# Additive attention on one core: other engines for the slots' relus, and a new order of scores, maxima and sums

## The chip, the cores and the metric

The kernel runs as one program on one core of a Trainium2 chip. The metric is device time in microseconds (us). PE is TensorE, DVE VectorE, ACT ScalarE, POOL GpSimd, SP SyncE.

## The reference, cut to what matters

The whole program is two layers of an adaLN network. The change touches only the attention of layer 1, on X of 4 batches x 1024 tokens x 256 channels, with 64 features (A = 64):

```python
q = jnp.einsum('bnc,ac->bna', X, Wq)
k = jnp.einsum('bnc,ac->bna', X, Wk)
Vy = jnp.einsum('bnc,dc->bnd', X, Wy_w) + Wy_b
e = jax.nn.relu(_rho_signed_sqrt(q[:, :, None, :] + k[:, None, :, :]))
scores = jnp.einsum('bija,a->bij', e, Wphi)
m = jnp.max(scores, axis=-1, keepdims=True)
ex = jnp.exp(scores - m)
denom = jnp.sum(ex, axis=-1)
part1 = jnp.einsum('bij,bjc->bic', ex, Vy)
Ew = jnp.einsum('bij,bija->bia', ex, e)
part2 = jnp.einsum('bia,ca->bic', Ew, We_w) + We_b * denom[..., None]
return (part1 + part2) / (denom[..., None] + EPS_DEN)
```

For every pair (i, j) of tokens and every feature, e is the root of the relu of q + k. It is used twice: for the scores, and, weighted with ex, for Ew.

## The kernel before

**Tiles and slots.** A tile is 32 queries (TI = 32) against all 1024 keys of the batch. It has 16 slots (NP = 16), each of two queries: partitions are 2 queries x 64 features, and a slot is 1024 keys wide. There are 128 tiles, four (q = 0 to 3) to a group of 128 queries, 32 to a batch. `e_slots` holds two tiles (`par` = q % 2). While tile t is worked on by DVE, tile t+1 gets its last roots and its scores, and tile t+2 gets its relus and first root.

**What each tile costs each engine.** The relu of a slot, relu(k + q), is made by the engine that `Z_BY` names: V, DVE in one instruction (L753, five slots, all issued in a burst behind slot 15 by `Z_AFTER`); A, ACT in one (L575, four slots); P, POOL in two, a clamp (L680) and an addition (L686), seven slots. A relu for tile t+2 overwrites the slot of tile t, so it waits for DVE's multiply of that slot. ACT then takes roots of four slots at a time (L584, four per tile; root s covers slots 4s to 4s+3 and waits for all four relus), and once per tile loads the exponential's table, takes ex from the scores and the negative maximum (L591), and loads the root's table again. POOL splits ex in two parts (`parts`, L666 and L668), which PE needs for all broadcasts of the next tile.

**PE and DVE, slot by slot.** PE's `tile` runs over the slots n of tile t: two matmuls broadcast ex (L493) into one of two PSUM buffers (`spread`), for which broadcast n waits for multiply n-2; then come the quarters of scores that `SCORES_AT[n]` lists, each 4 matmuls in 8 passes of 256 columns (L452). Quarters 4s to 4s+3 need root s. Entries `(1, ...)` are of tile t+1, `(2, ...)` of tile t+2. Once per tile PE turns ex (L499) at slot `EXT_AT` (0) or, for q = 0, at `EXT_AT_FIRST`; ACT copies it out (`turned`), for q = 0 DVE (L805). In q = 3 and the next q = 0, PE adds the group's eight products with the values, at the slots in `SUMS_LAST` and `SUMS_NEXT`; in q = 1 it turns the group's output back at slot `TURN_AT`, for which ACT's `normed` must have run. DVE multiplies slot by slot (L798, reads the broadcast and `e_slots`, and accumulates Ew), takes the maximum of tile t+1 in three steps behind slots `MAX_AT` to `MAX_AT + 2` (L760, L765, L770), ends a group in q = 0 and q = 1 (L778, L780, L786), and takes over the next batch's keys and queries at a seam (`next_batch`, three times in all).

Each engine runs its instructions in the order written; all waits are on semaphores (`sqrt_done`, `xb_freed`, `bc_done`, `scores_done`, `max_done`, `exp_done`, `parts_done`).

**Order in the loops.** ACT's step: root 3 of t+1, `turned`, relus of slots 2 and 3, root 0 and relu of slot 6 (all of t+2), exponential of t+1, relu of slot 10, roots 1 and 2 of t+2. POOL's step: queries of the tile (L690), relus in pairs (0, 1), (4, 5), (7, 8), `parts`, relu of slot 9.

Of the kernel before, what the change touches and what calls it, by code (L numbers as in the profile page):

```python
# [10 lines left out]
P = 128  # L11
# [27 lines left out]
NP = TI // 2  # L39
# [5 lines left out]
GT = 4  # L45
# [40 lines left out]
def adaln_kernel(nc, a, out):  # L86
# [9 lines left out]
    Z_BY = "PPAAPPAPPPAVVVVV"  # L96
    Z_AFTER = {15: [11, 12, 13, 14, 15]}


    EXT_AT, EXT_AT_FIRST, MAX_AT, TURN_AT = 0, 13, 8, 4  # L100

    SUMS_LAST, SUMS_NEXT = {9: 1, 14: 1, 15: 2}, {0: 1, 8: 1, 9: 1, 10: 1}
# [3 lines left out]
    SCORES_AT = {1: (1, (4, 5, 6, 7, 8)), 2: (1, (9,)), 3: (1, (10,)), 4: (1, (11,)), 5: (1, (12,)), 6: (1, (13,)), 7: (1, (14,)),  # L106
                 8: (1, (15,)), 10: (2, (0,)), 11: (2, (1,)), 12: (2, (2,)), 13: (2, (3,))}
    SCORES_AT_FIRST = SCORES_AT | {1: (1, (4, 5, 6, 7)), 2: (1, (8,)), 3: (1, (9, 10))}
# [18 lines left out]
    with ctx:  # L127
# [268 lines left out]
        TILES, GROUPS, N_SUMS = B * NTI, B * NG, JT  # L396
# [42 lines left out]
        def pe_c(pe):  # L439
# [45 lines left out]
            def tile(t, q, first=False, last=False, sums_of=None, values=None, more_sums_of=None, turn=None):  # L485
# [4 lines left out]
                for n in range(NP):  # L490
# [4 lines left out]
                    if n == (EXT_AT if q else EXT_AT_FIRST):  # L495
                        pe.wait_ge(ext_copied, t + 1)
                        for j in range(JT):
                            half, block = divmod(j, JT // BPB)
                            turned_ = nc.tensor.matmul(banks[:, 6, j * TI:(j + 1) * TI],  # L499
                                                       ex_parts[:, par, block * P:(block + 1) * P],  # L500
                                                       c_["selt"][:, half, :], start=True, stop=True)
                        turned_.then_inc(ext_mm, 1)
# [6 lines left out]
                    ahead, ms = (SCORES_AT if q else SCORES_AT_FIRST).get(n, (0, ()))  # L509
# [55 lines left out]
        def act_c(act):  # L565
# [26 lines left out]

            def first_root(t, par, freed):
                for n in (2, 3):
                    relu(t, par, n, freed)
                sqrt(t, par, 0)
                relu(t, par, 6, freed)

            def next_roots(t, par, freed):
                relu(t, par, 10, freed)  # L600
                nc.scalar.preload_act_table(ACT.Sqrt)  # L601
                sqrt(t, par, 1)
                sqrt(t, par, 2)

            def last_root(t, par):
                sqrt(t, par, 3)
# [6 lines left out]
            def turned(t, q):  # L613

                act.wait_ge(ext_mm, t + 1)
                nc.scalar.activation(ex_t_of[:, :, :, q, :], turned_ex, ACT.Copy).then_inc(ext_copied, 1)

            def step(t, q):

                par = q % 2  # L620
                last_root(t + 1, 1 - par)
                if q:
                    turned(t, q)
                first_root(t + 2, par, t * NP)
                ex_of(t + 1, 1 - par)
                next_roots(t + 2, par, t * NP)
# [4 lines left out]
            for n in (2, 3, 6):  # L631
                relu(1, 1, n, None)
            ex_of(0, 0)
            relu(1, 1, 10, None)
            nc.scalar.preload_act_table(ACT.Sqrt)
            for s in range(3):
                sqrt(1, 1, s)
            step(0, 0)
            step(1, 1)
            with act.Fori(0, GROUPS - 1) as tg:  # L640
                step(tg * GT + 2, 2)
                step(tg * GT + 3, 3)
                step(tg * GT + GT, 0)
                normed(tg)
                step(tg * GT + (GT + 1), 1)
            last_root(TILES - 1, 1)
            turned(TILES - 2, 2)
            ex_of(TILES - 1, 1)
# [12 lines left out]
        def pool_c(pool):  # L661
# [32 lines left out]
            pool.wait_ge(z_v, Z_BY.count("V"))  # L694
            pool.sem_inc(z_clamped, Z_BY.count("P"))
            some_z(1, 1, (0, 1), None)
            some_z(1, 1, (4, 5), None)
            parts(0, 0)
            some_z(1, 1, (7, 8), None)
            some_z(1, 1, (9,), None)  # L700

            def step(t, par, tl=None, last=False):

                if not last:
                    tile_queries(tl, par)
                    some_z(t + 2, par, (0, 1), t * NP)
                    some_z(t + 2, par, (4, 5), t * NP)
                    some_z(t + 2, par, (7, 8), t * NP)
                pool.wait_ge(bc_done, t * NP)
                parts(t + 1, 1 - par)  # L710
                if not last:
                    some_z(t + 2, par, (9,), t * NP)
# [18 lines left out]
        def dve_c(dve, own):  # L731
# [58 lines left out]
            def step(t, q, more=True, ends=None, seam=None, adds=None):  # L790

                par = q % 2
                if seam is not None:
                    next_batch(seam)
                for n in range(NP):
# [5 lines left out]
                    if ends is not None and n == EXT_AT_FIRST:  # L801
                        group_end(ends, 0)
                    if q == 0 and n == EXT_AT_FIRST + 1:
                        dve.wait_ge(ext_mm, t + 1)
                        nc.vector.tensor_copy(ex_t_of[:, :, :, q, :], turned_ex).then_inc(ext_copied, 1)  # L805
                    if MAX_AT <= n < MAX_AT + 3 and (more or q == GT - 2):
                        row_max(t + 1, 1 - par, n - MAX_AT, 0 if q else -1)
                    if ends is not None and n == EXT_AT_FIRST + 1:
                        group_end(ends, 1)
                    if adds is not None and n == TURN_AT + 2:  # L810
                        group_end(adds, 2)
# [1855 lines left out]
```

## Time and profile before

| | us |
|---|---|
| Median of 3 runs (5036.22 to 5052.96) | 5045.31 |
| Span of the profiled execution | 5032.0 |
| PE busy | 4414.1 (88%) |
| DVE busy | 4019.8 (80%) |
| ACT busy | 3419.9 (68%) |
| POOL busy | 3163.8 (63%) |
| Attention stage, first to last multiply | about 1230 to 4303 |

The span is the program on the chip; the runs' times are somewhat longer. A row of the costliest groups reads: line, engine, operation, output<-input, shapes, count | busy us in all, mean ns of one | idle time of the engine just before them, and what ended most of it. In a timeline, consecutive instructions of one engine overlap by some 0.08 us, so that what one costs is the distance between two starts; two starts follow from one another in the rows. In a table of stretches each engine has its busy us and, in brackets, its number of instructions; behind them stand the granted clock of PE (1.00 is 2.4 GHz) and the DMA. "x5" after a row is five instructions merged, with the time of all.

### The profile page before, as it was taken

The page shows a single profiled execution, that of the slowest core. Times are in us where ns is not written, and L with a number is a line of the kernel's source. Part 1 is how long each engine was busy: PE and PEld are TensorE (multiplying, and loading weights), DVE is VectorE, ACT ScalarE, POOL GpSimd, SP SyncE. Part 2 cuts the span into 40 slices and gives each one's busy share as a digit, 9 for nine tenths or more (in the row PEclk, how much of TensorE's full clock was granted, in tenths as well). Part 3 has the DMA queues.
Part 4 walks back from the last instruction along what each step waited for, and adds up shares of the span by engine and source line. Part 5 has one row for each costly group of instructions (what it writes and reads, how often), then busy time and mean ns, then how long its engine had stood idle before and what let it go on. Part 6 is the DMA issues. An engine that isn't in the chain of part 4 may idle for free.

```text
span 5032.0 us, 83939 instructions
## 1 busy us (share of the span) xinstructions
PE 4414.1 (88%) x28586; PEld 2295.6 (46%) x28586; DVE 4019.8 (80%) x6598; ACT 3419.9 (68%) x2402; POOL 3163.8 (63%) x2716
## 2 busy tenths in 40 slices
PE   6888876887889888888988988898898888799998
PEld 3333333464334433434433433443443443577777
DVE  2789896535999999999999999999999999422225
ACT  2232221315999999999999999999999999444443
POOL 0666662534777777777777777777777777233334
PEclk8888887899999999999999999999999999999999
DMA  6000001352000000000000000000000000200002
GB/s 229 0 0 1 0 1 51 134 175 89 3 2 2 4 2 2 17 4 2 2 4 2 17 4 2 2 4 2 11 3 4 2 2 4 102 17 8 17 25 84
DMA packets 70482, 130.78 MB, mean 26 GB/s; under 512 B 8264, under 2 KB 46632, under 8 KB 65889
## 3 DMA queue, kind: packets, MB, share of 16 engines
q1 hardware_dynamic: 61152, 106.21, 6.2%
q0 software_dynamic: 9216, 23.17, 1.2%
q8 instruction: 58, 0.95, 0.1%
q14 instruction: 56, 0.45, 0.0%
HBM read 74.66 MB, written 61.03 MB: 27 GB/s over the span
## 4 chain that ended last, share of the span: by engine, by line
PE 30%; issue 23%; DVE 15%; ACT 14%; POOL 2%; DVEq 1%; DMA 0%; ACTq 0%; POOLq 0%; SPq 0%
ACT e_slots L584 11%; PE banks L2250 8%; PE banks L493 8%; DVE e_slots L798 7%; PE banks L452 7%; DVE e_slots L753 2%; ACT L601 1%; DVE ew L798 1%; POOL g_l L2380 1%; PE banks L1602 1%; ACT e_slots L575 1%; PE banks L465 1%; PE banks L289 1%; PE banks L1656 1%; PE banks L1553 1%
## 5 line engine op out<-in xcount | busy, mean ns | idle before, releaser
L798 DVE CUSTOM_DVE_ANT_0 e_slots<-e_slots,banks 128x1024 f32<-128x1024 f32 x2048 | 2445.5, 1217 | 101.9 <-PE banks L493 97.4
L584 ACT ACTIVATE e_slots<-e_slots 128x4096 f32<-128x4096 f32 x512 | 1841.0, 3620 | 72.1 <-DVE e_slots L753 43.0
L493 PE MATMUL banks<-ex_parts,sel 128*128 128x512 f32 x4096 | 1513.5, 452 | 165.5 <-DVE ew L798 156.2
L680 POOL TENSOR_SCALAR e_slots<-k,qt 128x1024 f32<-128x1024 f32 x889 | 993.6, 1119 | 686.5 <-DVE ew L798 628.5
L452 PE MATMUL banks<-e_slots,w_score 128*32 128x256 f32 x16384 | 1249.9, 397 | 167.2 <-ACT e_slots L584 160.8
L493 PEld LDWEIGHTS banks<-ex_parts,sel 128*128 128x128 f32 x4096 | 628.7, 189 | 905.8 <-DVE ew L798 732.7
L686 POOL TENSOR_SCALAR e_slots<-e_slots,qt 128x1024 f32<-128x1024 f32 x889 | 988.7, 1119 | 63.9 <-POOL e_slots L680 25.5
L452 PEld LDWEIGHTS banks<-e_slots,w_score 128*32 128x32 f32 x16384 | 374.5, 110 | 861.7 <-issue 560.6
L575 ACT ACTIVATE e_slots<-k,qt 128x1024 f32<-128x1024 f32 x508 | 565.9, 1139 | 3.4 <-DVE ew L798 3.3
L2380 POOL TENSOR_TENSOR g_l<-tmp,g_h 128x512 fp32r<-128x512 f32 x192 | 260.6, 1358 | 421.2 <-ACT g_h L2347 288.4
L753 DVE TENSOR_SCALAR e_slots<-k,qt 128x1024 f32<-128x1024 f32 x635 | 453.3, 779 | 0.0
L2250 PE MATMUL banks<-g_h,r_h 128*128 128x512 f32 x1024 | 406.6, 397 | 6.4 <-POOL g_l L2380 6.4
L1283 POOL TENSOR_TENSOR state<-state,r_ 128x1024 f32<-128x1024 f32 x128 | 294.3, 2302 | 184.7 <-DVE state L1383 183.9
L2250 PE MATMUL banks<-g_l,r_h 128*128 128x512 f32 x1024 | 400.3, 391 | 0.0
L1383 DVE TENSOR_TENSOR_SCAN state<-decay,banks 128x1024 f32<-128x1024 f32 x128 | 292.3, 2284 | 4.4
L2346 ACT ACTIVATE tmp<-banks,r_sh 128x512 f32<-128x512 f32 x128 | 88.3, 690 | 269.8 <-PE banks L2250 269.7
L2250 PEld LDWEIGHTS banks<-g_h,r_h 128*128 128x128 f32 x1024 | 193.3, 189 | 51.3 <-POOL g_l L2380 9.0
L591 ACT ACTIVATE ex<-banks,negmax 128x512 f32<-128x512 f32 x128 | 88.2, 689 | 184.9 <-DVE negmax L770 184.9
L2250 PEld LDWEIGHTS banks<-g_l,r_h 128*128 128x128 f32 x1024 | 193.4, 189 | 43.3 <-issue 3.4
L2405 DVE RECIPROCAL r_std<-r_std 128x512 f32<-128x512 f32 x7 | 23.5, 3353 | 218.8 <-ACT r_std L2314 218.8
L668 POOL TENSOR_TENSOR ex_parts<-ex,part 128x512 fp32r<-128x512 f32 x128 | 164.3, 1283 | 10.7
L1013 PE MATMUL banks<-v_parts,spread 128*128 128x512 f32 x256 | 112.7, 528 | 65.9 <-DVE state L1383 65.1
(341 smaller groups left out, 5006.4 us busy)
## 6 DMA issues: line engine op xcount, KB each, us to landing
stage<-in_h SPq DMA_DIRECT2D x16, 1024.0 KB, 4.8
moe_slots<-empty_slot SPq DMA_DIRECT2D x1, 10320.0 KB, 36.2
slots<-moe_slots SPq DMA_DIRECT2D x8, 1290.0 KB, 6.9
moe_out<-empty_slot SPq DMA_DIRECT2D x1, 8192.0 KB, 56.4
two_rows<-moe_out SPq DMA_DIRECT2D x16, 512.0 KB, 5.8
stage<-in_w SPq DMA_DIRECT2D x6, 1024.0 KB, 6.3
x_tokens<-in_x SPq DMA_DIRECT2D x1, 4096.0 KB, 18.9
w_down<-in_w_down SPq DMA_DIRECT2D x1, 4096.0 KB, 12.9
```

The lines of the kernel that those rows point to most:

```text
L452: ins = nc.tensor.matmul(banks[TI * g:TI * (g + 1), par, side * QW:(side + 1) * QW], c_["w_score"][:, s, half, :], e_slots[:, par, COLG * ...
L493: ins = nc.tensor.matmul(spread[n % 2][:, half * W:(half + 1) * W], c_["sel"][:, half, n, :], ex_parts[:, par, :], start=True, stop=True)
L575: nc.scalar.activation(e_slots[:, par, n, :], k2[:, :], ACT.Relu, bias=qt[:, par, 0, place(n):place(n) + 1]).then_inc(z_a, 1)
L584: nc.scalar.activation(e_slots[:, par, four, :], e_slots[:, par, four, :], ACT.Sqrt, bias=EPS_RHO).then_inc(sqrt_done, 1)
L680: nc.gpsimd.tensor_scalar(e_slots[:, par, n, :], k2[:, :], FLT_MAX, qt[:, par, 1, place(n):place(n) + 1], ALU.min, ALU.max).then_inc(z_cla ...
L686: nc.gpsimd.tensor_scalar(e, e, qt[:, par, 0, place(n):place(n) + 1], 1.0, ALU.add, ALU.mult).then_inc(z_p, 1)
L753: nc.vector.tensor_scalar(e_slots[:, par, n, :], k2[:, :], qt[:, par, 0, place(n):place(n) + 1], 0.0, ALU.add, ALU.max).then_inc(z_v, 1)
L798: nc.vector.tensor_tensor_reduce(out=e, in0=e, in1=spread[n % 2], scale=1.0, scalar=0.0, op0=ALU.mult, op1=ALU.add, accum_out=ew[:, q, pla ...
L1283: nc.gpsimd.tensor_tensor(state, state, r_[:, b % 2, n // N, :], ALU.mult).then_inc(pr_done, 1)
L1383: nc.vector.tensor_tensor_scan(st[:, s % RING, 1:T + 1], dk[:, c, :], kv, 0.0, ALU.mult, ALU.add).then_inc(scan_done, 1)
L2250: ins = nc.tensor.matmul(dst, w_[w][:, k, o * P:(o + 1) * P], x[:, k, :], start=k == 0 and part_ == 0, stop=k == n_k - 1 and part_ == 1)
L2380: nc.gpsimd.tensor_tensor(w_[lo][:, o, :], tmp[:, o % N_TMP, :], w_[hi][:, o, :].bitcast(fp32), ALU.subtract).then_inc(lo_done, 1)
```

## The change

Seven relus stay with POOL, four with ACT and five with DVE, but on other slots: POOL 0, 1, 3, 4, 6, 9, 15; ACT 2, 5, 7, 14; DVE 8, 10, 11, 12, 13 (still one burst behind slot 15). POOL makes them in threes (0, 1, 3), (4, 6, 9), then `parts`, then 15. ACT takes only root 1 behind the exponential; roots 2 and 3, with relu 14 between them, come in the next step, behind `turned` and, where there is one, `normed`. The maxima go from behind slots 8, 9, 10 to 10, 11, 12. The scores of t+1 end at slot 10 instead of 8, those of t+2 come at slots 12, 13 and 15, and slots 0, 2, 6, 11 and 14 have none. The eight sums, the turning for q = 0, the turning back and DVE's group ends move, and the batch's hand-over goes behind slot 4. PE waits for the next tile's maximum before it turns ex in q = 0.

```diff
-    Z_BY = "PPAAPPAPPPAVVVVV"
-    Z_AFTER = {15: [11, 12, 13, 14, 15]}
-    EXT_AT, EXT_AT_FIRST, MAX_AT, TURN_AT = 0, 13, 8, 4
-    SUMS_LAST, SUMS_NEXT = {9: 1, 14: 1, 15: 2}, {0: 1, 8: 1, 9: 1, 10: 1}
-    SCORES_AT = {1: (1, (4, 5, 6, 7, 8)), 2: (1, (9,)), 3: (1, (10,)), 4: (1, (11,)), 5: (1, (12,)), 6: (1, (13,)), 7: (1, (14,)),
-                 8: (1, (15,)), 10: (2, (0,)), 11: (2, (1,)), 12: (2, (2,)), 13: (2, (3,))}
-    SCORES_AT_FIRST = SCORES_AT | {1: (1, (4, 5, 6, 7)), 2: (1, (8,)), 3: (1, (9, 10))}
+    Z_BY = "PPAPPAPAVPVVVVAP"
+    Z_AFTER = {15: [8, 10, 11, 12, 13]}
+    EXT_AT, EXT_AT_FIRST, MAX_AT, TURN_AT, SEAM_AT = 0, 14, 10, 1, 4
+    SUMS_LAST, SUMS_NEXT = {1: 1, 2: 1, 12: 1, 14: 1, 15: 3}, {11: 1}
+    SCORES_AT = {1: (1, (4, 5, 6, 7)), 3: (1, (8,)), 4: (1, (9,)), 5: (1, (10,)), 7: (1, (11,)), 8: (1, (12,)), 9: (1, (13,)),
+                 10: (1, (14, 15)), 12: (2, (0,)), 13: (2, (1,)), 15: (2, (2, 3))}
...
                         pe.wait_ge(ext_copied, t + 1)
+                        if not q:
+                            pe.wait_ge(max_done, t + 2)
...
-                    ahead, ms = (SCORES_AT if q else SCORES_AT_FIRST).get(n, (0, ()))
+                    ahead, ms = SCORES_AT.get(n, (0, ()))
...
+            def late_roots(t, par, freed):
+                sqrt(t, par, 2)
+                relu(t, par, 14, freed)
+                sqrt(t, par, 3)
+
             def first_root(t, par, freed):
-                for n in (2, 3):
+                for n in (2, 5):
                     relu(t, par, n, freed)
                 sqrt(t, par, 0)
-                relu(t, par, 6, freed)
-
-            def next_roots(t, par, freed):
-                relu(t, par, 10, freed)
+                relu(t, par, 7, freed)
+
+            def second_root(t, par):
                 nc.scalar.preload_act_table(ACT.Sqrt)
                 sqrt(t, par, 1)
-                sqrt(t, par, 2)
...
                 par = q % 2
-                last_root(t + 1, 1 - par)
                 if q:
                     turned(t, q)
+                if done is not None:
+                    normed(done)
+                late_roots(t + 1, 1 - par, (t - 1) * NP if not isinstance(t, int) or t else None)
                 first_root(t + 2, par, t * NP)
                 ex_of(t + 1, 1 - par)
-                next_roots(t + 2, par, t * NP)
+                second_root(t + 2, par)
...
                     tile_queries(tl, par)
-                    some_z(t + 2, par, (0, 1), t * NP)
-                    some_z(t + 2, par, (4, 5), t * NP)
-                    some_z(t + 2, par, (7, 8), t * NP)
+                    some_z(t + 2, par, (0, 1, 3), t * NP)
+                    some_z(t + 2, par, (4, 6, 9), t * NP)
                 pool.wait_ge(bc_done, t * NP)
                 parts(t + 1, 1 - par)
                 if not last:
-                    some_z(t + 2, par, (9,), t * NP)
+                    some_z(t + 2, par, (15,), t * NP)
...
-                if seam is not None:
-                    next_batch(seam)
                 for n in range(NP):
...
+                    if seam is not None and n == SEAM_AT:
+                        next_batch(seam)
-                    if ends is not None and n == EXT_AT_FIRST:
+                    if ends is not None and n == MAX_AT + 2:
                         group_end(ends, 0)
-                    if q == 0 and n == EXT_AT_FIRST + 1:
+                    if q == 0 and n == EXT_AT_FIRST:
...
-                    if ends is not None and n == EXT_AT_FIRST + 1:
+                    if ends is not None and n == EXT_AT_FIRST:
                         group_end(ends, 1)
-                    if adds is not None and n == TURN_AT + 2:
+                    if adds is not None and n == TURN_AT:
                         group_end(adds, 2)
```

## Rows read from the trace of the kernel before

**Rows 1.** The page's part 5: costliest groups of instructions, columns as described above.

```profile
L798 DVE CUSTOM_DVE_ANT_0 e_slots<-e_slots,banks 128x1024 f32<-128x1024 f32 x2048 | 2445.5, 1217 | 101.9 <-PE banks L493 97.4
...
L584 ACT ACTIVATE e_slots<-e_slots 128x4096 f32<-128x4096 f32 x512 | 1841.0, 3620 | 72.1 <-DVE e_slots L753 43.0
...
L680 POOL TENSOR_SCALAR e_slots<-k,qt 128x1024 f32<-128x1024 f32 x889 | 993.6, 1119 | 686.5 <-DVE ew L798 628.5
```

**Rows 2.** Busy time of each engine in one group of four tiles.

```profile
core 0: us, PE busy (x) PEld busy (x) DVE busy (x) ACT busy (x) POOL busy (x), PEclk, DMA share, GB/s
2525.00:2620.80 95.80, 84.99 (x696) 38.47 (x696) 93.32 (x170) 88.22 (x49) 72.14 (x68) 1.00 0.01 3
```

**Rows 3.** Timeline of DVE: start us, us, instruction, [idle before <-releaser]; next group's copy.

```profile
2221.01 0.42 DVE L805 COPY ex_t<-banks 128x256 f32<-128x256 f32 x1
```

**Rows 4.** Timeline of DVE, from a tile's five relus to the next tile's.

```profile
2150.75 3.42 DVE L753 TENSOR_SCALAR e_slots<-k,qt 128x1024 f32<-128x1024 f32 x5
...
2154.09 1.21 DVE L798 CUSTOM_DVE_ANT_0 e_slots<-e_slots,banks 128x1024 f32<-128x1024 f32 x1
...
2156.80 1.22 DVE L798 CUSTOM_DVE_ANT_0 e_slots<-e_slots,banks 128x1024 f32<-128x1024 f32 x1 [0.36 <-PE banks L493]
...
2165.34 0.69 DVE L760 TENSOR_REDUCE half_max<-banks 128x1 f32<-128x512 f32 x1
...
2165.95 1.21 DVE L798 CUSTOM_DVE_ANT_0 e_slots<-e_slots,banks 128x1024 f32<-128x1024 f32 x1
...
2168.29 0.15 DVE L770 TENSOR_TENSOR negmax<-half_max,banks 128x1 f32<-128x1 f32 x1
...
2169.50 1.22 DVE L798 CUSTOM_DVE_ANT_0 e_slots<-e_slots,banks 128x1024 f32<-128x1024 f32 x1
...
2170.64 1.22 DVE L798 CUSTOM_DVE_ANT_0 e_slots<-e_slots,banks 128x1024 f32<-128x1024 f32 x1
...
2174.07 3.73 DVE L753 TENSOR_SCALAR e_slots<-k,qt 128x1024 f32<-128x1024 f32 x5
```

**Rows 5.** Timeline of DVE in the tiles q = 0 and q = 1.

```profile
2124.07 1.22 DVE L798 CUSTOM_DVE_ANT_0 e_slots<-e_slots,banks 128x1024 f32<-128x1024 f32 x1 [0.73 <-PE banks L493]
...
2125.22 0.42 DVE L805 COPY ex_t<-banks 128x256 f32<-128x256 f32 x1
...
2139.22 0.61 DVE L786 SCALAR_TENSOR_TENSOR xg<-banks,gate_g,xg 128x128 f32<-128x128 f32 x2
```

**Rows 6.** Timeline of PE: broadcasts (L493), quarters of scores (L452).

```profile
2108.64 1.07 PE L452 MATMUL banks<-e_slots,w_score 128*32 128x256 f32 x16
...
2127.55 1.93 PE L452 MATMUL banks<-e_slots,w_score 128*32 128x256 f32 x32
...
2131.36 0.64 PE L452 MATMUL banks<-e_slots,w_score 128*32 128x256 f32 x8 [1.87 <-ACT e_slots L584]
...
2131.93 0.73 PE L493 MATMUL banks<-ex_parts,sel 128*128 128x512 f32 x2
...
2132.59 0.64 PE L452 MATMUL banks<-e_slots,w_score 128*32 128x256 f32 x8
```

**Rows 7.** Timeline of ACT: two exponentials in a row, a table load between.

```profile
2145.22 0.69 ACT L591 ACTIVATE ex<-banks,negmax 128x512 f32<-128x512 f32 x1 [1.61 <-DVE negmax L770]
...
2146.96 1.28 ACT L601 ACT_TABLE_LOAD   x1
...
2168.54 0.69 ACT L591 ACTIVATE ex<-banks,negmax 128x512 f32<-128x512 f32 x1 [1.20 <-DVE negmax L770]
```

**Rows 8.** Timeline of DVE, then POOL, at the start of the stage.

```profile
1213.98 3.40 DVE L753 TENSOR_SCALAR e_slots<-k,qt 128x1024 f32<-128x1024 f32 x5
...
1214.48 4.98 POOL L680 TENSOR_SCALAR e_slots<-k,qt 128x1024 f32<-128x1024 f32 x2 [16.47 <-DVE e_slots L831]
```

**Rows 9.** Timeline of POOL in the loop, and at a batch's end.

```profile
2170.77 1.28 POOL L668 TENSOR_TENSOR ex_parts<-ex,part 128x512 fp32r<-128x512 f32 x1
...
2174.55 0.66 POOL L690 COPY qt<-q_pairs 128x32 f32 x1
...
2730.96 0.21 POOL L690 COPY qt<-q_pairs 128x32 f32 x1 [5.20 <-DVE q_pairs L744]
```

More of the change, by code:

```diff
@@ L591, in ex_of @@
                 nc.scalar.activation(ex[:, :], bank(par), ACT.Exp, bias=negmax[:, 0:1]).then_inc(exp_done, 1)
+            def late_roots(t, par, freed):
+                sqrt(t, par, 2)
+                relu(t, par, 14, freed)
+                sqrt(t, par, 3)
             def first_root(t, par, freed):
-                for n in (2, 3):
+                for n in (2, 5):
                     relu(t, par, n, freed)
                 sqrt(t, par, 0)
-                relu(t, par, 6, freed)
-            def next_roots(t, par, freed):
-                relu(t, par, 10, freed)
+                relu(t, par, 7, freed)
+            def second_root(t, par):
                 nc.scalar.preload_act_table(ACT.Sqrt)
                 sqrt(t, par, 1)
-                sqrt(t, par, 2)
-            def last_root(t, par):
-                sqrt(t, par, 3)
             def normed(tg):
@@ L616, in turned, with step @@
                 nc.scalar.activation(ex_t_of[:, :, :, q, :], turned_ex, ACT.Copy).then_inc(ext_copied, 1)
-            def step(t, q):
+            def step(t, q, done=None):
                 par = q % 2
-                last_root(t + 1, 1 - par)
                 if q:
                     turned(t, q)
+                if done is not None:
+                    normed(done)
+                late_roots(t + 1, 1 - par, (t - 1) * NP if not isinstance(t, int) or t else None)
                 first_root(t + 2, par, t * NP)
                 ex_of(t + 1, 1 - par)
-                next_roots(t + 2, par, t * NP)
+                second_root(t + 2, par)
             for s in range(PER):
                 sqrt(0, 0, s)
-            for n in (2, 3, 6):
+            for n in (2, 5, 7):
                 relu(1, 1, n, None)
             ex_of(0, 0)
-            relu(1, 1, 10, None)
             nc.scalar.preload_act_table(ACT.Sqrt)
-            for s in range(3):
+            for s in range(2):
                 sqrt(1, 1, s)
@@ L643, in act_c @@
                 step(tg * GT + GT, 0)
-                normed(tg)
-                step(tg * GT + (GT + 1), 1)
-            last_root(TILES - 1, 1)
+                step(tg * GT + (GT + 1), 1, done=tg)
             turned(TILES - 2, 2)
+            late_roots(TILES - 1, 1, (TILES - 3) * NP)
             ex_of(TILES - 1, 1)
@@ L694, in pool_c @@
             pool.wait_ge(z_v, Z_BY.count("V"))
+            pool.wait_ge(z_p, Z_BY.count("P"))
             pool.sem_inc(z_clamped, Z_BY.count("P"))
-            some_z(1, 1, (0, 1), None)
-            some_z(1, 1, (4, 5), None)
+            some_z(1, 1, (0, 1, 3), None)
+            some_z(1, 1, (4, 6, 9), None)
             parts(0, 0)
-            some_z(1, 1, (7, 8), None)
-            some_z(1, 1, (9,), None)
+            some_z(1, 1, (15,), None)
             def step(t, par, tl=None, last=False):
```

## The prediction

> **What bounds the kernel now.** I read the timelines of one group of four tiles, engine by engine, because the shares of the whole span mix stages. The group repeats: DVE's copy of the turned ex comes at 2125.22 and again at 2221.01 [rows 3, 5], a round of 95.8 us. Counting the maxima over the stage gives the same 95.8 for all groups but three at 97.2 (PE at a lower clock for some microseconds) and three with a batch's end (1.3 to 2.8 more). In one such group DVE is busy 93.3 us, ACT 88.2, PE 85.0, POOL 72.1, at full clock [rows 2]. DVE is the bound, though not a perfect one: its multiplies stand idle 101.9 us in all, 97.4 of it for PE's broadcasts [rows 1], and gaps under a tenth of a microsecond come on top. They show as pace: back to back four multiplies take 2174.07 - 2169.50 = 4.57, so 1.143 each [rows 4]; beside PE slots with a broadcast and a quarter of scores the pace is PE's, 2132.59 - 131.36 = 1.23 [rows 6].
>
> Two things make PE late. First, behind slot 1 it stands at the quarter that needs root 2: 1.87 us in vain [rows 6], then DVE waits at slot 2 (0.36 in [rows 4]). Second, quarters in seven slots running let PE fall back 0.09 a slot. In q = 0 PE's turning of ex at slot 13, right behind DVE, adds 0.73 [rows 5], and in q = 1 the turning back comes on top of a slot that already has a quarter.
>
> **The bare DVE round.** 16 multiplies x 1.143 = 18.28. The maximum costs 2165.95 - 2165.34 = 0.61 and its two small steps 0.07 each (they overlap their neighbours): 0.75. The burst costs 2154.09 - 2150.75 = 3.34 [rows 4]. Sum 22.37 a tile, 89.5 a group. Group ends add 0.5 (two additions, 0.61 long), 0.34 (copy, 0.42 long) and 0.15 (two small ones, estimate) [rows 5]: 90.5. So 5.3 of 95.8 is loss, of which the change can take away all or nothing. The counts per engine (7, 4, 5 relus, 4 roots) stay, so the sum of DVE's work doesn't move; only the loss does.
>
> **Part 1, roots 2 and 3 behind `turned`; scores thinned out.** I walk a tile of q = 2 or 3, with 0 at DVE's first multiply. Multiply 10 starts at 10 x 1.143 = 11.4; behind it come the maximum (1.14 + 0.61), multiply 11, the small step, multiply 12 (each 1.14 + 0.07), so the negative maximum runs from 15.5 to 15.7 and the exponential starts at 15.77 (today 2168.54 - 2168.29 = 0.25 behind the last step's start [rows 4, 7]). ACT: table, root 1 (3.62, 3.53 from start to start) done at 21.3; `turned`; root 2 done at 25.1, that is 2.7 in the next tile; relu 14; root 3 done at 7.4; relus 2 and 5; root 0 starts at 9.7, done 13.2; relu 7; table; ready at 15.7. ACT's round without waits is 2168.54 - 2145.22 - 1.20 = 22.12 today [rows 7]; with relu 14 between two roots I take 22.2, so it fits in 22.37 with 0.1 to 0.2 to spare (q = 1 adds `normed`, about 0.36, but DVE has 0.5 more there). PE: quarters 4 to 7 start with root 1 at 21.3 and take 1.9 [rows 6], done at 23.2; broadcast 2 may start at 23.6 anyway. Quarter 8 is met at 3.1 (root 2: 2.7), quarter 12 at 8.8 (root 3: 7.4), quarter 0 at 13.7 (root 0: 13.2). No root is late, so PE's wait of 1.87 is gone, and DVE's wait at slot 2 with it.
>
> Broadcast n+2 may start 0.06 behind multiply n's end and needs 0.77 to DVE's start, so PE may be 0.24 late before DVE notices. This room is an estimate from the distances in the timelines. Three quarters in a row make 3 x 0.09 = 0.27, and a free slot (0.66 for the broadcast) resets it: 0.03 lost behind slots 5 and 9. The double quarter at slot 10 (1.0, from 1.07 in [rows 6]) lies beside the maximum's 0.61: none lost. In q = 0 the turning at slot 14 (0.8) loses about 0.06, where now it is 0.73. The new wait for `max_done` there has the next broadcast queued behind it, but the maximum is done at 15.8 and PE comes at 16.4: nothing. The three sums at slot 15 and the turning back at slot 1 lie beside the burst (3.34): nothing; without that cover 1.0 and 0.5. Group: 90.5 + 4 x 0.06 + 0.06 = 90.8. If my 0.24 of room is not there, each run of three costs its 0.27: 0.54 a tile, group 92.7.
>
> **Part 2, POOL's threes and slot 15.** Relu 15 can't start before multiply 15, which is when DVE's burst starts. Such a clamp stands in the trace once: given at 1214.48 beside DVE's burst of 1213.98 to 1217.38, two clamps took 4.98 instead of 2.24, so the first ended at 1218.35, 0.97 behind the burst, while the burst kept its 3.40 [rows 8]. So I take: POOL waits out the burst, DVE loses nothing. Then from the burst's end: rest of clamp 1.0, gap 0.2, addition 1.1, queries and gaps 0.45, three clamps 3.33, gap 0.1, three additions 3.33: 9.5. Root 0 wants them at 9.7. It fits by 0.2. The second three ends at 16.4, the exponential at 16.5; `parts` 16.7 to 18.75; DVE's burst starts at 19.0, POOL's slack 0.3. POOL's round is then full, where the clamps stood idle 686.5 us [rows 1]. Today POOL's addition for slot 9 runs into the burst and holds its first relu up, 3.73 instead of 3.42 for five [rows 4]; that 0.3 goes in most tiles and is already in the bare round.
>
> The Trainium skill, "SBUF — State Buffer", section "Who interferes with whom", says that DVE in a 2-port mode (its `tensor_scalar` can be one) and GpSimd exclude each other, and that whoever issues first has the shared ports for the whole instruction. It speaks of one instruction, not of a burst of five: by it POOL's clamp might come in between two relus. The clamp of the start did not.
>
> **Part 3, seams and ends.** The hand-over behind slot 4 (three times; today POOL waits 5.20 for it, [rows 9]) starts POOL's threes at 7.9 instead of 3 or so; root 0 and the exponential come some 3.5 late, and so does the next tile: 1.5 + 3.2 = 4.7 each, 14 in all against 6.9 now: +7. At the stage's start POOL makes six relus before the first `parts` instead of four, about +4.5, of which the first tiles give most back: +1.
>
> **Sum.** 31 groups x (95.8 - 90.8) = 155; -155 + 8 = -147. On the profiled execution 5032 - 147 = 4885; the median stands 13 above that span: 4898. Ends: without any PE loss (90.5) -164 + 8, 4889, and a few less if the groups of 97.2 go: 4880. With 0.54 a tile, -96 + 8: 4957.
>
> **Rivals.**
> A, POOL and ACT late (a new wait for the removed one). Slacks of 0.1 to 0.3 in three places are less than one gap of POOL. If the clamp behind the burst costs a whole unit more (1.1), POOL's chain burst, slots 0, 1, 3, root 0, exponential, `parts`, next burst is 18.6 + 3.3 + 1.1 = 23.0: 0.6 more a tile, 2.5 a group, 31 x 2.5 = 78: 4976. For: the chain is closed and 21.9 long already. Against: [rows 8] measures the delay.
> B, slower: POOL gets in between DVE's relus. Its place is the burst, in every tile. POOL's copy of the queries, waiting at the first relu, needed 0.66 instead of 0.21 [rows 9], so it came in behind one relu; if the clamp (1.11) and the addition (1.12) do likewise, the burst grows by 2.2. Group 90.8 + 8.9 = 99.7, 31 x 3.9 = 121, + 8: 5174. The clamp alone: 95.3, about 5038. It decides for slower from 1.3 us a tile of POOL's work inside the burst. Against: the clamp of [rows 8], the same instruction. That is what the page's rule would give if locks were handed over at each instruction.
> C, PE's waits move and don't shrink: a root misses its quarter by half a microsecond (0.4 to 0.5 of room at quarters 8 and 0), each time 0.3 to 0.5 for DVE: up to 1 a tile, 5022 (124 back).
>
> **How the numbers follow.** Forecast (4880 to 4957) 0.65; A 0.17; C 0.07; B with both instructions 0.06, with the clamp alone 0.05. The likeliest is 4898. Range 4875 to 4980: it takes in A and leaves out C and B, 0.18 together. A measurement of this kernel can't tell less than 0.3% (15 us). Slower: B with both 0.06, 0.01 of the rest; within: B's clamp alone and a third of C, 0.06; faster 0.87.
>
> **What would show it.** Right: a group round near 91; no wait of PE for L584 behind slot 1; DVE's multiplies idle under 25 us in all; the clamp of slot 15 some 4 us long behind the burst; the burst at 3.4. A shows as ACT's root 0 waiting for POOL and no wait of the exponential for the maximum; B as a burst of 5 us or more; C as PE waiting for L584. The prediction is wrong if `parts` slips behind the burst's start: it then waits out the whole burst, and the next tile starts some 2 us late.

## The result, and the profile after

The changed kernel takes 5166.82 us (median of 4 runs, 5155.82 to 5175.6) against 5049.14 (5036.22 to 5059.44): ratio 1.0238, 95% interval 1.0218 to 1.0258. It is slower by 118 us, where 147 us less were forecast. The profiled execution has a span of 5163.0 us against 5032.0.

From the page, the busy line and three groups (line, engine, operation, count | busy us, mean ns of one | idle before, releaser), which answer to [rows 1]:

```profile
PE 4455.2 (86%) x28586; PEld 2326.0 (45%) x28586; DVE 4160.2 (81%) x6598; ACT 3438.4 (67%) x2402; POOL 3240.4 (63%) x2716
...
L796 DVE CUSTOM_DVE_ANT_0 e_slots<-e_slots,banks 128x1024 f32<-128x1024 f32 x2048 | 2391.6, 1213 | 79.4 <-PE banks L492 78.4
...
L681 POOL TENSOR_SCALAR e_slots<-k,qt 128x1024 f32<-128x1024 f32 x889 | 1032.0, 1163 | 670.1 <-DVE ew L796 623.4
...
L753 DVE TENSOR_SCALAR e_slots<-k,qt 128x1024 f32<-128x1024 f32 x635 | 649.2, 1086 | 0.0
```

PE's lateness did go down: the idle time before DVE's multiplies fell from 101.9 to 79.4 us. But DVE's own relus (L753), 635 before and after, now take 649.2 us, 1086 ns each by the page; the same 635 took 453.3 us before, 779 each. This is the engine that bounds the stage. The round of one group of four tiles, from DVE's copy of the turned ex to the next, in the form of [rows 2]:

```profile
core 0: us, PE busy (x) PEld busy (x) DVE busy (x) ACT busy (x) POOL busy (x), PEclk, DMA share, GB/s
2240.90:2340.00 99.10, 86.28 (x697) 39.34 (x697) 97.64 (x170) 88.77 (x49) 74.60 (x69) 0.98 0.01 3
```

99.1 us instead of 95.8, with DVE busy 97.6 of it. DVE's timeline, which answers to [rows 4]:

```profile
2293.19 5.12 DVE L753 TENSOR_SCALAR e_slots<-k,qt 128x1024 f32<-128x1024 f32 x5
...
2298.24 1.21 DVE L796 CUSTOM_DVE_ANT_0 e_slots<-e_slots,banks 128x1024 f32<-128x1024 f32 x1
...
2303.46 1.22 DVE L796 CUSTOM_DVE_ANT_0 e_slots<-e_slots,banks 128x1024 f32<-128x1024 f32 x1 [0.58 <-PE banks L492]
...
2305.37 1.22 DVE L796 CUSTOM_DVE_ANT_0 e_slots<-e_slots,banks 128x1024 f32<-128x1024 f32 x1 [0.68 <-PE banks L492]
```

A burst of five is 5.12 us long instead of 3.42 (3.73 where POOL's addition ran into it). And POOL beside it, which answers to [rows 8, 9]:

```profile
2293.50 1.42 POOL L681 TENSOR_SCALAR e_slots<-k,qt 128x1024 f32<-128x1024 f32 x1 [0.61 <-DVE ew L796]
...
2295.12 1.33 POOL L687 TENSOR_SCALAR e_slots<-e_slots,qt 128x1024 f32<-128x1024 f32 x1 [0.20 <-POOL e_slots L681]
...
2296.40 0.66 POOL L691 COPY qt<-q_pairs 128x32 f32 x1
```

The clamp comes 0.31 us behind the burst's start and takes 1.42, not some 4; the addition takes 1.33. So POOL is not kept out: it comes in between the relus, twice. Taken one by one in the trace, the relus start at 0, 0.67, 2.20, 3.73 and 4.38 us, and the second and third last 1.61 each instead of 0.75. Each of POOL's two instructions costs DVE 0.87. All 126 bursts of the loop look like this one.

The last two rows of DVE are a second effect, in one tile of most groups. PE's timeline of that place and two stretches of the group (columns as above):

```profile
2299.51 0.74 PE L492 MATMUL banks<-ex_parts,sel 128*128 128x512 f32 x2 [1.95 <-DVE ew L796]
...
2301.32 0.96 PE L451 MATMUL banks<-e_slots,w_score 128*32 128x256 f32 x8
...
2302.20 1.22 PE L492 MATMUL banks<-ex_parts,sel 128*128 128x512 f32 x2
...
2303.36 1.08 PE L451 MATMUL banks<-e_slots,w_score 128*32 128x256 f32 x8
```

```profile
2297.50:2301.00 3.50, 1.15 (x8) 0.60 (x4) 3.50 (x7) 3.50 (x2) 1.31 (x2) 1.00 0.00 0
2301.00:2304.40 3.40, 3.40 (x21) 0.90 (x19) 2.82 (x5) 3.29 (x2) 2.14 (x3) 0.57 0.00 0
```

PE stands idle 1.95 us beside the longer burst; less than two microseconds later a quarter of scores takes 0.96 to 1.08 instead of 0.64 and a broadcast 1.22 instead of 0.73, at a granted clock of 0.57 on the mean, between full speed (2.4 GHz) and half (1.2 GHz). Such a tile is 25.5 us long instead of 24.1.

The sum fits the measured round: 90.8 as forecast for the new order, + 4 x 1.70 = 97.6, + 1.45 for that tile = 99.05; measured 99.1. Over 31 groups that is 31 x 8.3 = 257 us on top of the 147 less: +110, against 131 between the spans. Of the 21 us that are left, 10 don't belong to the change: DVE's first relu of the stage comes at 1213.46 instead of 1203.38, and over all runs of this study this moment lies between 1201 and 1215, behind the same code. So two spans should not be compared more closely than that. Most of the rest is six groups of 101.1 to 101.4 us with a granted clock of 0.95, where the kernel before has three of 97.2 to 97.3 between its seams. The three groups with a seam are 6.2, 4.6 and 4.6 longer than their neighbours, 1.4, 2.8 and 2.8 before: 8.4 more, of which 7 are in the forecast already.

### The profile page after: what moved, and what is told of

Same layout as the page of the kernel before. It is cut to its first block, busy times and chain, and to the rows that moved or that the text cites. A ratio compares the mean times of both kernels' runs of the same rounds, so it can differ in the third digit from the quotient of the medians.

```text
span 5163.0 us, 83882 instructions
## 1 busy us (share of the span) xinstructions
PE 4455.2 (86%) x28586; PEld 2326.0 (45%) x28586; DVE 4160.2 (81%) x6598; ACT 3438.4 (67%) x2402; POOL 3240.4 (63%) x2716
## 4 chain that ended last, share of the span: by engine, by line
DVE 44%; issue 19%; PE 17%; POOL 3%; DVEq 1%; ACT 1%; DMA 0%; POOLq 0%; SPq 0%; ACTq 0%
DVE e_slots L796 27%; DVE e_slots L753 10%; PE banks L2250 6%; PE banks L492 2%; DVE ew L796 2%; POOL g_l L2380 2%; PE banks L451 2%; PE banks L1602 1%; DVE half_max L760 1%; PE banks L288 1%; PE banks L1553 1%; PE banks L1656 1%; PE banks L1665 1%; DVEq L794 0%; PE banks L1587 0%
## 5 line engine op out<-in xcount | busy, mean ns | idle before, releaser
L796 DVE CUSTOM_DVE_ANT_0 e_slots<-e_slots,banks 128x1024 f32<-128x1024 f32 x2048 | 2391.6, 1213 | 79.4 <-PE banks L492 78.4
L681 POOL TENSOR_SCALAR e_slots<-k,qt 128x1024 f32<-128x1024 f32 x889 | 1032.0, 1163 | 670.1 <-DVE ew L796 623.4
L451 PE MATMUL banks<-e_slots,w_score 128*32 128x256 f32 x16384 | 1207.8, 396 | 73.2 <-ACT e_slots L585 73.1
L492 PEld LDWEIGHTS banks<-ex_parts,sel 128*128 128x128 f32 x4096 | 640.6, 193 | 1149.3 <-DVE ew L796 930.5
L687 POOL TENSOR_SCALAR e_slots<-e_slots,qt 128x1024 f32<-128x1024 f32 x889 | 1010.3, 1148 | 51.2 <-POOL e_slots L681 25.5
L451 PEld LDWEIGHTS banks<-e_slots,w_score 128*32 128x32 f32 x16384 | 392.8, 110 | 725.0 <-issue 482.2
L753 DVE TENSOR_SCALAR e_slots<-k,qt 128x1024 f32<-128x1024 f32 x635 | 649.2, 1086 | 0.0
```

What stands on the lines that cost most here:

```text
L451: ins = nc.tensor.matmul(banks[TI * g:TI * (g + 1), par, side * QW:(side + 1) * QW], c_["w_score"][:, s, half, :], e_slots[:, par, COLG * ...
L492: ins = nc.tensor.matmul(spread[n % 2][:, half * W:(half + 1) * W], c_["sel"][:, half, n, :], ex_parts[:, par, :], start=True, stop=True)
L681: nc.gpsimd.tensor_scalar(e_slots[:, par, n, :], k2[:, :], FLT_MAX, qt[:, par, 1, place(n):place(n) + 1], ALU.min, ALU.max).then_inc(z_cla ...
L687: nc.gpsimd.tensor_scalar(e, e, qt[:, par, 0, place(n):place(n) + 1], 1.0, ALU.add, ALU.mult).then_inc(z_p, 1)
L753: nc.vector.tensor_scalar(e_slots[:, par, n, :], k2[:, :], qt[:, par, 0, place(n):place(n) + 1], 0.0, ALU.add, ALU.max).then_inc(z_v, 1)
L796: nc.vector.tensor_tensor_reduce(out=e, in0=e, in1=spread[n % 2], scale=1.0, scalar=0.0, op0=ALU.mult, op1=ALU.add, accum_out=ew[:, q, pla ...
```

## The experiments

All times are medians; the kernel before took 5039.74 to 5042.96 beside them. The diffs are against the changed kernel, unless said otherwise.

### POOL behind the burst, and other arrivals

```diff
                 if not last:
+                    pool.wait_ge(z_v, (t + 3) * Z_BY.count("V"))
+                    pool.sem_inc(pool_begun, 1)
                     some_z(t + 2, par, (15,), t * NP)
```

> The change, but POOL's relu of slot 15 waits until all five relus of DVE's burst are done. Theory T (POOL's two instructions enter DVE's burst, and each holds it up 0.87 us): the burst is back at 3.4 us instead of 5.12, the group round falls from 99.1 us to 91 to 92.5, the time to 4890 to 4960. Rival A (POOL's chain is too long: the change would be slow without the collision, too): burst 3.4 us, but root 0 waits for POOL, group 93.5 or more, time 4980 or more. Rival K (the tile in each group with PE at half clock is a cost of the new order itself): it stays, 1.45 us a group, 45 us in all.

Measured: 4898.75 us (ratio to before 0.9713, 0.9689 to 0.9737). One group, and the burst, POOL's clamp and ACT's root 0:

```profile
2327.29:2418.32 91.03, 84.27 (x704) 39.17 (x696) 90.68 (x170) 88.34 (x49) 70.63 (x69) 1.00 0.01 3
```

```profile
2421.81 3.40 DVE L755 TENSOR_SCALAR e_slots<-k,qt 128x1024 f32<-128x1024 f32 x5
...
2425.61 1.12 POOL L681 TENSOR_SCALAR e_slots<-k,qt 128x1024 f32<-128x1024 f32 x1 [4.02 <-DVE e_slots L755]
...
2435.30 3.63 ACT L585 ACTIVATE e_slots<-e_slots 128x4096 f32<-128x4096 f32 x1 [0.68 <-POOL e_slots L687]
```

The burst is back at 3.40, the round 91.0, and the tile at half clock is gone from all but six of the 31 groups (PE's clock 1.00 in the others). Theory T holds, and the collision with what follows from it is worth 268 us. ACT waits for POOL before root 0 (0.68 us), as rival A had it, but that wait is nearly covered (91.0 against 90.8 in the next kernel): the chain has just room enough.

Left out altogether:

```diff
                 if not last:
-                    some_z(t + 2, par, (15,), t * NP)
+                    pool.wait_ge(xb_freed, t * NP + (15 + 3))
+                    pool.sem_inc(z_clamped, 1)
+                    pool.sem_inc(z_p, 1)
```

> The change without POOL's relu of slot 15 (that slot keeps stale data; its two counts are raised behind multiply 15). No collision and 2.2 us less work on POOL in each tile. Theory T: group 90.8 to 91.2, time 4890 to 4910; the difference to the kernel in which POOL waits out the burst is what that wait costs. Rival A: as fast as T here, but the kernel that waits is over 60 us slower.

Measured: 4887.45 us; a group takes 90.79, the forecast's 90.8. Waiting out the burst costs 11 us by the medians, 31 x 0.24 = 7 by the groups.

Then the question why POOL was kept out at the start of the stage [rows 8] and not here. First, the waits within the burst, and an additional clamp of slot 0 that doesn't wait for DVE's first relus:

```diff
-                if freed is not None:
-                    dve.wait_ge(xb_freed, freed + (n + 3))
-                dve.wait_ge(qt_ready, t + 1)
+                if n == Z_AFTER[15][0]:
+                    dve.wait_ge(qt_ready, t + 1)
+                    if freed is not None:
+                        dve.wait_ge(xb_freed, freed + (15 + 3))
...
+            pool.wait_ge(qt_ready, 2)
+            nc.gpsimd.tensor_scalar(e_slots[:, 1, 0, :], k2[:, :], FLT_MAX, qt[:, 1, 1, place(0):place(0) + 1],
+                                    ALU.min, ALU.max).then_inc(warm, 1)
+            pool.wait_ge(warm, 1)
+            pool.sem_inc(pool_begun, 1)
             pool.wait_ge(z_v, Z_BY.count("V"))
```

> The change, but only the first relu of DVE's burst has waits (for multiply 15 and the queries), the other four follow without any; and at the stage's start POOL makes one more clamp of slot 0, before it waits for DVE's first relus. Theory W (at the start of the stage POOL was kept out of a burst because the relus there had no wait on the multiplies): the burst is 3.4 us again, POOL's clamp some 4 us long, time about 4900 to 4960. Theory I (POOL gets in behind any relu that it finds running): the burst stays 5.1 us, time 5150 to 5180. For the start: if the 3.85 us of the first clamp was the wait for the burst, the clamp that comes second stays at 3.8 us; if it was a first use, the additional clamp takes that time and the second one 1.1 to 1.5 us, and then it lies inside the burst.

Measured: 5182.93 us, the burst 5.1: theory W falls. The start of the stage, DVE and POOL:

```profile
1202.69 11.55 DVE L838 TENSOR_SCALAR e_slots<-k,qt 128x1024 f32<-128x1024 f32 x16 [7.08 <-POOLq L280]
...
1214.16 3.40 DVE L760 TENSOR_SCALAR e_slots<-k,qt 128x1024 f32<-128x1024 f32 x5
...
1202.93 1.49 POOL L697 TENSOR_SCALAR e_slots<-k,qt 128x1024 f32<-128x1024 f32 x1 [5.59 <-POOLq L280]
...
1214.54 6.18 POOL L681 TENSOR_SCALAR e_slots<-k,qt 128x1024 f32<-128x1024 f32 x3 [10.12 <-DVE e_slots L838]
```

The additional clamp comes 0.24 us behind the first of 16 relus and gets in behind it (1.49 us; DVE's 16 take 11.55 instead of 10.69, as they do in the kernel that waits out the burst: the 0.87 again). The next one comes at the seventeenth relu and is kept out over the four that follow: three clamps 6.18 us. So neither a first use nor the waits explain [rows 8].

Then the moment at which POOL comes. In the first kernel one wait and two raised semaphores more delay it:

```diff
                 if not last:
+                    pool.wait_ge(xb_freed, t * NP + (15 + 3))
+                    for _ in range(2):
+                        pool.sem_inc(pool_begun, 1)
                     some_z(t + 2, par, (15,), t * NP)
```

> The change, but POOL raises a semaphore twice more between its wait for multiply 15 and its clamp, so that the clamp comes some 0.2 us later than the 0.30 us behind the start of DVE's first relu at which it comes in the change. Theory P (whether POOL gets in hangs on where in the running relu it comes: at 0.20 to 0.31 us behind its start it gets in behind it, at 0.38 to 0.53 us, as at the start of the stage in three kernels, it is kept out to the end of the burst): burst 3.4 us, clamp about 4 us long, time 4885 to 4910. Rival (in the loop POOL always gets in behind the relu it finds running): burst 5.1, time 5150 to 5180.

Measured: 5166.95 us. Burst, clamp and addition:

```profile
2296.12 5.13 DVE L756 TENSOR_SCALAR e_slots<-k,qt 128x1024 f32<-128x1024 f32 x5
...
2296.62 1.23 POOL L681 TENSOR_SCALAR e_slots<-k,qt 128x1024 f32<-128x1024 f32 x1 [0.81 <-DVE ew L799]
...
2298.05 1.32 POOL L687 TENSOR_SCALAR e_slots<-e_slots,qt 128x1024 f32<-128x1024 f32 x1 [0.20 <-POOL e_slots L681]
```

The clamp comes 0.50 us into the first relu and still goes in behind it, and 0.50 is also what lay between relu and clamp in [rows 8]: theory P falls. The next three let POOL wait for the first, the second or the third relu:

```diff
                 if not last:
+                    pool.wait_ge(z_v, (t + 2) * Z_BY.count("V") + 1)
+                    pool.sem_inc(pool_begun, 1)
                     some_z(t + 2, par, (15,), t * NP)
```

> The change, but POOL's clamp of slot 15 waits for the first relu of DVE's burst, so that it comes about 0.3 us behind the start of the second. Theory P: it gets in behind the second one, and its addition behind the third: burst 5.1 us, time 5150 to 5190. Rival (POOL gets in only behind a burst's first relu): burst 3.4 us, time 4885 to 4910.

Measured: 5190.61 us, from two executions that lie far apart (5164.8 and 5216.43; the trace is of the first). In the other two the 1 is a 2 and a 3. They were put on record together: "the kernel before this one" is the one that waits for the third relu, and theory Q is stated with that one.

> As the kernel before this one, but POOL waits for the second relu and comes during the third. Theory Q: it gets in behind the fourth, only the fifth is held up: burst 4.3 us, group 91.0 + 4 x 0.87 = 94.5, time 5000 to 5020, more if tiles at the lower clock come back. Rival (behind any running relu): the fourth and the fifth are held up, burst 5.1, 5150 to 5180. Rival (kept out from here on): 4885 to 4900.

Measured: 4985.01 us.

> The change, but POOL's clamp of slot 15 waits for the third relu of DVE's burst, so that it comes during the fourth. Theory Q (POOL waits for those of DVE's relus that are already handed on when it comes, and DVE hands them on ahead: at its first relu none, at the second one more, deep in a long burst several): the fifth is ahead of it, the burst stays 3.4 us, the clamp ends about 1.0 us behind the burst; time 4885 to 4900, if anything a little under the 4898.75 us of the kernel that waits for all five. Rival (only the relu that runs is waited for): the fifth is held up, burst 4.3 us, 0.87 a tile, 5000 to 5020.

Measured: 4880.38 us (ratio to before 0.9687, 0.9664 to 0.9711). The bursts and POOL's clamps of the three, in this order:

```profile
2303.45 5.05 DVE L755 TENSOR_SCALAR e_slots<-k,qt 128x1024 f32<-128x1024 f32 x5
...
2304.59 1.83 POOL L681 TENSOR_SCALAR e_slots<-k,qt 128x1024 f32<-128x1024 f32 x1 [1.45 <-DVE e_slots L755]
```

```profile
2299.04 4.18 DVE L755 TENSOR_SCALAR e_slots<-k,qt 128x1024 f32<-128x1024 f32 x5
...
2300.85 1.83 POOL L681 TENSOR_SCALAR e_slots<-k,qt 128x1024 f32<-128x1024 f32 x1 [2.58 <-DVE e_slots L755]
```

```profile
2304.01 3.40 DVE L755 TENSOR_SCALAR e_slots<-k,qt 128x1024 f32<-128x1024 f32 x5
...
2306.47 1.83 POOL L681 TENSOR_SCALAR e_slots<-k,qt 128x1024 f32<-128x1024 f32 x1 [2.77 <-DVE e_slots L755]
...
2308.51 1.13 POOL L687 TENSOR_SCALAR e_slots<-e_slots,qt 128x1024 f32<-128x1024 f32 x1 [0.20 <-POOL e_slots L681]
```

Coming 1.14 us behind the burst's start, in the second relu, POOL is done at 2.97, so it began at 1.86 (1.11 earlier), when the third relu was half through: one relu went ahead of it, the third, and the fourth was held up by 0.78. Its addition holds up the fifth by 0.87. Coming in the third it waits for the fourth and holds up only the fifth, by 0.78 (4.18). Coming in the fourth it waits for the fifth, and nothing is held up (3.40). Theory Q fits what was seen in all of these: ahead of POOL goes what DVE has already handed on, which is a reading and not measured. Measured is the number of relus that go ahead beyond the running one: none at a burst's first, one at the second and third, at least one at the fourth (the burst has no sixth), at least four at the seventeenth. What in DVE sets this number wasn't tested. The time of the kernel that came third (4985 against 5000 to 5020 expected) is under the range, because only 0.78 and not 0.87 is lost per tile, and on top of a round of 90.8 and not 91.0: 93.9 a group and not 94.5.

The kernel in which POOL waits for the third relu is the best of this study, 162 us faster than the kernel before. Its round and groups:

```profile
2322.87:2413.65 90.78, 84.38 (x702) 39.02 (x696) 90.59 (x170) 88.14 (x48) 73.44 (x69) 1.00 0.01 3
```

```profile
L798 DVE CUSTOM_DVE_ANT_0 e_slots<-e_slots,banks 128x1024 f32<-128x1024 f32 x2048 | 2384.8, 1214 | 31.3 <-PE banks L492 30.7
...
L585 ACT ACTIVATE e_slots<-e_slots 128x4096 f32<-128x4096 f32 x512 | 1851.4, 3623 | 51.3 <-POOL e_slots L687 27.3
...
L755 DVE TENSOR_SCALAR e_slots<-k,qt 128x1024 f32<-128x1024 f32 x635 | 431.9, 747 | 0.0
```

### The collision put into the kernel before

```diff
                 if not last:
+                    pool.wait_ge(xb_freed, t * NP + (15 + 3))
+                    pool.sem_inc(pool_begun, 1)
                     some_z(t + 2, par, (9,), t * NP)
```

> The kernel before, but POOL's last relu (slot 9) waits for multiply 15, so that its clamp and addition fall on DVE's burst. Theory T: burst 5.1 us instead of 3.4 to 3.7, 1.5 us a tile more, 126 tiles: 190 us, less what the longer burst takes off the waits for roots (up to 1 us in the tiles q = 1 to 3): 5120 to 5240. Rival (the collision costs only together with the new order): under 5070.

Measured: 5470.1 us, 428 more than before and far above what was expected. The burst is 5.12 here as well, but that is the smaller part. ACT and PE:

```profile
2304.38 7.12 ACT L584 ACTIVATE e_slots<-e_slots 128x4096 f32<-128x4096 f32 x2 [2.16 <-POOL e_slots L686]
...
2308.05 1.08 PE L452 MATMUL banks<-e_slots,w_score 128*32 128x256 f32 x8 [3.84 <-ACT e_slots L584]
...
2309.06 1.22 PE L493 MATMUL banks<-ex_parts,sel 128*128 128x512 f32 x2
```

In the kernel before slot 9 belongs to root 2, and PE meets that root's first quarter in slot 1. ACT's root now waits 2.16 us for POOL, PE 3.84 for the root, and then runs at half the clock. The run shows that the collision doesn't need the new order; it gives no price for it, because the edit also made a root late.

### The order of the quarters, and the threes

Both are against the kernel that waits out the burst (4898.75).

```diff
-    SCORES_AT = {1: (1, (4, 5, 6, 7)), 3: (1, (8,)), 4: (1, (9,)), 5: (1, (10,)), 7: (1, (11,)), 8: (1, (12,)), 9: (1, (13,)),
-                 10: (1, (14, 15)), 12: (2, (0,)), 13: (2, (1,)), 15: (2, (2, 3))}
+    SCORES_AT = {1: (1, (4, 5, 6, 7)), 3: (1, (8,)), 4: (1, (9,)), 5: (1, (10,)), 6: (1, (11,)), 7: (1, (12,)), 8: (1, (13,)),
+                 9: (1, (14,)), 10: (1, (15,)), 12: (2, (0,)), 13: (2, (1,)), 14: (2, (2,)), 15: (2, (3,))}
```

> The kernel in which POOL waits out the burst (4898.75 us, group 91.0), with the quarters 8 to 15 in the slots 3 to 10 without a free slot between, and those of t+2 in slots 12 to 15. The pace theory of the prediction (a slot with a quarter takes PE 1.233 us, DVE 1.143, and PE may be 0.24 late): eight in a row make 0.72, so 0.48 lost in each tile, 0.42 more than now, 1.7 a group, 53 in all: 4940 to 4960. Rival (only the waits for roots mattered, not the order of the quarters): under 4910.

Measured: 4951.68 us (0.9819, 0.98 to 0.9839), 53 more. A group at full clock takes 92.4 instead of 91.0: the free slots are worth 1.4 a group, where the two paces say 1.7. The 1.4 make 43 us; nine groups have a granted clock below 1.00 here and six there, so not all of the 53 are the order's.

```diff
-                    some_z(t + 2, par, (0, 1, 3), t * NP)
-                    some_z(t + 2, par, (4, 6, 9), t * NP)
+                    some_z(t + 2, par, (0, 1), t * NP)
+                    some_z(t + 2, par, (3, 4), t * NP)
+                    some_z(t + 2, par, (6, 9), t * NP)
```

> The kernel in which POOL waits out the burst, with POOL's relus in pairs (0, 1), (3, 4), (6, 9) instead of threes. Slot 3's addition, for which root 0 waits, comes one instruction and a gap later, 1.2 us. If POOL's chain (burst, slots 0, 1, 3, root 0, exponential, parts, next burst) is as near the bound as the prediction's sum says (22.3 of 22.37 us), this costs 1.1 us in tiles q = 2 and 3 and 0.6 in q = 0 and 1, 3.4 a group, 105 in all: 4980 to 5040. Rival (the chain has more room than summed, the threes are idle): under 4920.

Measured: 5034.22 us, 135 more, at the upper end. ACT's root 0 now waits for POOL's addition of slot 3:

```profile
2400.48 3.62 ACT L585 ACTIVATE e_slots<-e_slots 128x4096 f32<-128x4096 f32 x1 [2.07 <-POOL e_slots L687]
```

The threes are no ornament: they bring slot 3 forward by one instruction, and POOL's chain has no more room than that. But the 135 us aren't all the chain's. Two groups (columns as above):

```profile
2122.97:2217.56 94.59, 83.72 (x697) 39.16 (x696) 91.83 (x172) 88.33 (x49) 70.72 (x69) 1.00 0.01 3
2407.89:2503.88 95.99, 86.75 (x697) 40.08 (x696) 91.21 (x172) 88.32 (x49) 70.73 (x69) 0.96 0.01 3
```

The first, at full clock, shows the chain's price: 94.6 - 91.0 = 3.6 a group, 112 in all, where 3.4 and 105 were worked out. Most groups are like the second: 0.6 to 1.4 longer at a granted clock of 0.96, though the burst is 3.4 us long here.

### PE's clock

The first of two kernels, which write the broadcast of slot 1 again:

```diff
-                    for half in range(2):
+                    for half in (0, 1) * (3 if n == 1 else 1):
```

> The change, with the broadcast of slot 1 written three times instead of once (four matmuls more, 1.3 us, in the time in which PE stands idle beside the burst). Theory C (the tile in each group at half the clock, 1.45 us, follows PE's idle time of 1.65 to 1.95 us beside the longer burst): these tiles go, group 97.6, time 5115 to 5135. Rival (the lower clock has another cause): time 5155 to 5180.

Measured: 5151.12 us. In the second, the number depends on the tile.

```diff
-                    for half in range(2):
+                    for half in (0, 1) * ((3, 2, 4, 4)[q] if n == 1 else 1):
```

> The change, with the broadcast of slot 1 written four times in the tiles q = 2 and 3, three times in q = 0 and twice in q = 1 (where the turning back follows and three times held PE up). Most of the remaining idle time beside the burst goes. Theory C (the tile at half the clock follows PE's idle time beside the burst): no such tile in most groups, group 97.6 to 97.9, time 5115 to 5135. Rival (another cause): a tile with 1.45 us more stays in each group, 5150 to 5180.

Measured: 5149.78 us. PE's waits beside the bursts in front of three tiles of one group of the second kernel, q = 1, 2 and 3:

```profile
2274.37 0.74 PE L492 MATMUL banks<-ex_parts,sel 128*128 128x512 f32 x2 [1.79 <-DVE ew L796]
...
2299.93 0.74 PE L492 MATMUL banks<-ex_parts,sel 128*128 128x512 f32 x2 [1.14 <-DVE ew L796]
...
2324.02 0.73 PE L492 MATMUL banks<-ex_parts,sel 128*128 128x512 f32 x2 [0.54 <-DVE ew L796]
```

In both kernels the slower tile is gone from q = 2 and has come up in q = 1, whose maxima then lie 26.0 us apart instead of 25.1. They gain 16 to 17 us instead of the 30 to 50 expected (two executions each): the waits got shorter, the slow tile stayed.

It is tempting to read that the low clock keeps to the tiles behind PE's longest wait. The first kernel's own trace speaks against it. PE in front of its tiles q = 1 and q = 2:

```profile
2270.42 0.74 PE L492 MATMUL banks<-ex_parts,sel 128*128 128x512 f32 x2 [1.45 <-DVE ew L796]
...
2272.44 1.08 PE L451 MATMUL banks<-e_slots,w_score 128*32 128x256 f32 x8
...
2295.97 0.74 PE L492 MATMUL banks<-ex_parts,sel 128*128 128x512 f32 x2 [1.59 <-DVE ew L796]
...
2297.77 0.64 PE L451 MATMUL banks<-e_slots,w_score 128*32 128x256 f32 x8
```

The tile behind 1.45 us is slow and the next one, behind 1.59, is not. In the changed kernel's group of above q = 1 is at full speed behind 1.78 and q = 2 slow behind 1.95. And the kernel with the pairs has a granted clock below 1.00 in 27 of its 31 groups, without a long burst. So theory C as it was put, with this one wait as the cause, doesn't hold, and its rival came nearer in the time. Shown is that the low clock is rarer in the kernels with neither the collision nor the pairs, that writing the broadcast again moves it to another tile, and what it costs there. What decides in which tile it comes stays open.

## Why the prediction was wrong, point by point

**The step that failed** is in part 2: "So I take: POOL waits out the burst, DVE loses nothing." It rested on one row, the clamp at the start of the stage [rows 8]. What the runs showed in its place: POOL's clamp and addition each go in between two relus of the burst, 0.87 us of DVE each, so that the burst takes 5.12 us and not 3.40 in every tile. The row was read rightly, but it stood behind 16 other relus, and the loop's clamp comes at the first of five. At that place no relu beyond the running one goes ahead of POOL (126 of 126 bursts). The sign was in [rows 9]: POOL's copy of the queries, waiting at a burst's first relu, was done 0.06 us behind that relu. The prediction weighed both and gave the row of the same instruction the greater weight (0.11 for rival B in all); the row of the same place in the loop was the nearer one. The page "SBUF — State Buffer" of the Trainium skill, section "Who interferes with whom", says of DVE's 2-port modes that whichever of the two engines issues first has the shared ports for its whole instruction while the other is fully blocked. The trace agrees for the single instruction: a relu that meets a clamp of 1.11 us lasts 1.61 instead of 0.75. It agrees less on who is next: a clamp that came 0.19 us before the third relu's start was done only at 2.97, with that relu ahead of it.

**Rival B** was the case that came, 5174 against 5166.82. That the times agree to 7 us is in part luck, since its terms were off in ways that cancel: the burst grew by 1.70 a tile, not 2.2, because a relu held up loses 0.87 and not the 1.11 of POOL's instruction; and 1.45 a group for PE's clock, which no part of the prediction had, came on top. The group is 99.1 and not 99.7; the 19 us of that were made up by the 10 from ahead of the stage and by the groups of 101.

**The bare round of DVE** (90.5) and **the new order's round** (90.8) held: 90.78 to 91.03 in three kernels without the collision. The forecast of 4898 is what the kernel that waits out the burst takes (4898.75), but to the microsecond that is luck: its span is 4894.9 and not 4885, and the median stands 4 above it and not 13. DVE's multiplies stand idle 42.4 us in all there and 31.3 in the best kernel, where under 25 were named. **Part 1** held term by term: no root is late beyond what is covered, and three quarters in a row lose nothing that shows; the price of a row of eight was measured, 1.4 us a group.

**Part 2's chain** held as a sum. It was thought to have 0.2 to spare; moving one addition back by 1.2 cost 3.6 us a group at full clock where 3.4 were worked out; with the lower clock it came to 135 us. Rival A did not come, even though the clamp behind the burst starts 0.4 and ends 1.52 us behind it, not the 1.0 of the sum, and root 0 waits 0.68 for POOL.

**Part 3.** In the best kernel the two distances of maxima at the first seam are 23.87 and 26.47 where 22.37 and 22.36 are usual: 5.6; at the second 4.8, at the third 4.9. 4.7 was forecast. Rival C did not come.

## What to carry to other kernels

Where two engines exclude each other by instruction, price a collision at the place in the burst at which it falls: a row from deep in a long burst says nothing on its first instruction. If one engine's work must fall beside the other's burst, the waiting side can be told to come late: here a wait for the third of five relus turned 118 us of loss into 162 of gain, with one semaphore wait. And look whether a row of a quite different instruction, but at the same place of the loop, contradicts the row that the forecast rests on.

## What the runs showed of the hardware that was not expected

How many relus of DVE go ahead of a waiting POOL instruction grows along a burst: none beyond the running one at the first relu, one at the second and third, at least four at the seventeenth. A POOL instruction of 1.11 us that gets in behind the running relu holds DVE up by 0.87, and by 0.78 where another relu had gone ahead of it. And a wait of PE of 1.95 us beside the longer burst, in a stage with PE busy 86 of 99 us, was followed by a stretch at half the clock that made its tile 1.45 us longer. No single wait tells where it comes: a tile behind 1.45 us was slow, tiles behind 1.59 and 1.78 were not.
